# Layer 2 of a four-layer graph kernel: unread products in the two places where TensorE waits

## The chip, the cores and the metric

The kernel runs on one core of one Trainium2 chip. The metric is the device time of one execution in microseconds (us), lower is better. The runs of the kernel before took 1992.58, 1993.73 and 1993.85 us.

## The reference

Four graph layers are computed one after another on 3125 nodes with 256 features and 53125 edges sorted by destination. Each is followed by `x = layernorm(x + layer(x))`. Layer 0 is a normalised graph convolution, layer 1 a weighted sum with two weight matrices, layer 3 a weighted sum after one matrix. Layer 2 is graph attention with four heads of 64 features:

```
z = einsum('nd,hdf->nhf', h, W)
e = leaky_relu(es[src] + ed[dst]);  e = where(e == 0, -1000, e)
m = segment_max(e, dst);  ex = exp(e - m[dst])
denom = segment_sum(ex, dst);  alpha = ex / denom[dst]
out = segment_sum(alpha * z[src], dst)
```

## The kernel before

Every engine has its own hand-written program, and semaphores order them. Layers 0, 1 and 3 go through a dense adjacency matrix, and TensorE multiplies it tile by tile (L1163, L1219). **Layer 2** is different. The edges are taken in 84 groups of 640: 128 partitions by 5 columns (KC = 5). A group touches a window of 48 destination nodes, so four heads make 192 columns (HW).

For one group, GpSimd (POOL in the profile) issues five indirect DMAs (L462), which fetch 128 rows each of the table of transformed source nodes into one of five slots of `ring`. It waits for `slot_free` first, which TensorE raises on the last of its sums for the group that used the slot. VectorE (DVE) makes one-hot matrices (L914) and logits (L920 to L939), masks them (L946), takes the maximum over the columns of each partition (L954), over the partitions (L960), and the running maximum (L969); it subtracts it (L979) and later adds the sums to the accumulator (L1000). ScalarE (ACT) copies the transposed one-hots (L567) and takes the exponentials (L580, L583).

TensorE's loop is software-pipelined. In iteration g, in this order (L1292 to L1305), it does:

- `transpose_max(g)`, L1268, 2 records: turns the partition maxima. It waits for `vmax_ready`, which is DVE's L954. DVE's L960 waits for it.
- `transpose_hots(g + 2)`, L1250, 5 records of 128 bf16 columns. ACT's L567 waits for it.
- `spread_max(g)`, L1277, 4 records. It waits for `mg_ready`, which is DVE's L960 of the same group, and for `mnew_ready` of the group before (L969).
- `sums(g - 1)`, head 0, L1287, 10 records.
- `destination_logits(g + 2)`, L1259, 5 records.
- `sums(g - 1)`, heads 1 to 3, L1287, 30 records. The last raises `slot_free`.

DVE's loop runs beside it in iteration g: masked (L946), new maximum of g - 1 (L969), partition maximum of g (L954), change of the maximum (L975), one-hots of g + 2 (L914), shift (L979), logits (L920), keep (L984), logits (L926), group maximum of g (L960), logits and rescale (L930, L992, L935, L939), add_sums of g - 2 (L1000).

PSUM banks: the sums of group k go to columns 0 to 191 of `sum_banks[k % 3]`, and the spread maximum to columns 0 to 191 of `mb_bank`. Columns 256 to 511 of these banks hold nothing in layer 2. `ident16` is the 128 by 128 identity in bf16.

Of the kernel before, what the change touches and what calls it, by code (L numbers as in the profile page):

```python
# [14 lines left out]
P = 128  # L15
WIN = 48
KC = 5
SLOTS = 5
# [5 lines left out]
NPAN = P // PAN  # L24
HALF = NPAN // 2
QUAD = 4
PAIR = 2
QUADS = NPAN // QUAD
HQ = QUADS // 2
HP = HALF // PAIR  # L30
GRAN = 16
# [8 lines left out]
def gnn_program(nc, x, src, dst, edge_weight, w0, b0, w_rel, b_rel, w_root, w_att, att, w3, b3, out):  # L40
    N, D = x.shape
    E = src.shape[0]
    H, _, F = w_att.shape
# [24 lines left out]
    with ctx:  # L68
        def sb(name, shape, dt=F32):
            return ctx.enter_context(nc.sbuf_tensor(name, shape, dt))  # L70

        def sem(name):
            return ctx.enter_context(nc.semaphore(name))
# [9 lines left out]
        ident16 = sb("ident16", [P, P], BF16)  # L83
# [54 lines left out]
        def carver(whole):  # L138
            at = [0]

            def carve(parts, *dims, dt=F32):
                n = int(np.prod(dims))
                words = n if dt in (F32, I32) else -(-n // 2)
                v = whole[0:parts, at[0]:at[0] + words]
                at[0] += words
                if dt != F32:
                    v = v.bitcast(dt)[:, 0:n]
                if len(dims) > 1:
                    names = "abcdef"[:len(dims)]
                    v = v.rearrange(f"p ({' '.join(names)}) -> p {' '.join(names)}", **dict(zip(names, dims)))  # L150
                return v
            return carve
# [44 lines left out]
        carve(P, NPAD)  # L197
        iota2 = carve(P, P, PAIR, dt=BF16)
        digs = [carve(P, 5, HALF, dt=BF16) for _ in range(2)]
# [7 lines left out]
        carve = carver(work)  # L207
        oh = [(carve(P, HP, P, PAIR, dt=BF16), carve(P, HP, NT * PAN, PAIR, dt=BF16),
               carve(P, 3, HP, NT * PAN, PAIR, dt=BF16)) for _ in range(2)]

# [22 lines left out]
        sum_banks = (banks[0], banks[1], banks[7])  # L233
        ed_bank, vmaxT_bank, mb_bank = banks[4], banks[5], banks[6]
# [35 lines left out]
        y = {n: sem(f"L2_{n}") for n in (  # L270
            "slot_free", "hot_ready", "added", "based", "moved", "relok", "pen_ready", "hotT_ps", "hotT_ready", "ed_ps", "lg",
            "val_ready", "vmax_ready", "vmaxT", "mg_ready", "mb", "mnew_ready", "dm_ready", "rm_ready",
            "shifted", "resc_ready", "prob_ready", "accmul")}
# [7 lines left out]
        def has(g):  # L281
            return 0 <= g < GROUPS

        def uses(r, g):
            return r * len(range(g % SLOTS, GROUPS, SLOTS)) + g // SLOTS + 1
# [119 lines left out]
        def _(pool):  # L405
            G = nc.gpsimd
            G.iota(ident[:], [[1, P]], base=0, channel_multiplier=-1, allow_small_or_imprecise_dtypes=True)
            G.iota(iota2, [[1, P], [0, PAIR]], base=0, channel_multiplier=0,
                   allow_small_or_imprecise_dtypes=True)
# [58 lines left out]
        def _(act):  # L468
# [34 lines left out]
            def counts(i, q):  # L503
                act.wait_ge(c_quad, i * QUADS + (q + 1))
                S.copy(ac[:, :, q * QUAD * PAN:(q + 1) * QUAD * PAN],  # L505
                       cnt_banks[q % 2][:, 0:NT * QUAD * PAN].rearrange("p (b d) -> p b d", b=NT)).then_inc(c_cev, 1)

# [106 lines left out]
        def _(dve):  # L614
# [60 lines left out]
            def numbers(width):  # L675
                return iota2[:, 0:width].unsqueeze(1).to_broadcast([P, HP, width, PAIR])

# [124 lines left out]
            def add_weights(t, i, q, r):  # L802
                dve.wait_ge(c_quad, i * QUADS + (q + 1))
                dve.wait_ge(c_wad, i * QUADS + (q + 1))
                part = aw[t % 2][:, :, q * QUAD * PAN:(q + 1) * QUAD * PAN]
                V.scalar_tensor_tensor(out=part, in0=part, scalar=keep[:, bass.ds(r, 1)],  # L806
                                       in1=w_banks[q % 2][:, 0:NT * QUAD * PAN].rearrange("p (b d) -> p b d", b=NT),
                                       op0=ALU.mult, op1=ALU.add).then_inc(c_wad, 1)
# [250 lines left out]
        def _(pe):  # L1059
            mm = nc.tensor.matmul  # L1060
# [13 lines left out]
            for c in range(CGRP):  # L1074
                ins = mm(banks[5][0:NPAN, 0:NT], gq_lo[:, c, :], gq_hi[:, c, :], start=(c == 0), stop=(c == CGRP - 1),
                         skip_group_check=True)
# [16 lines left out]
            for m, w in enumerate((wrel_r, wroot_r)):  # L1093
# [11 lines left out]
               start=True, stop=True).then_inc(s_bb, 1)  # L1105
# [36 lines left out]
            def adjacency(i, q):  # L1142
# [5 lines left out]
                lo, code, wtd = oh[h]  # L1148
                for k in range(QUAD):
                    cols = slice(k * PAN, (k + 1) * PAN)  # L1150
# [38 lines left out]
            for t in range(NT + 2):  # L1189
                if t < NT:  # L1190
                    if t >= 2:
                        pe.wait_ge(e0["u"], t - 1)
                    for j in range(3):
                        mm(out_banks[t % 2][:, 0:D], ident16[:, :], y0p[:, t, j, :], start=(j == 0), stop=False,
                           skip_group_check=True)
# [44 lines left out]
            def attention_products(r):  # L1240
                def number(k):
                    return r * GROUPS + k

                def transpose_hots(k):
                    s, i = k % SLOTS, number(k)
                    pe.wait_ge(y["hot_ready"], i + 1)
                    pe.wait_ge(y["hotT_ready"], i + 1)
                    pe.sem_inc(held, 1)
                    for c in range(KC):
                        ins = T(hotT_bank[:, c, 0:EP], hot16[:, s, c, :], ident16[0:EP, 0:EP])  # L1250
                    ins.then_inc(y["hotT_ps"], 1)

                def destination_logits(k):
                    s, i = k % SLOTS, number(k)
                    pe.wait_ge(y["hotT_ready"], i + 2)
                    pe.wait_ge(edw_loaded[s], 16 * uses(r, k))
                    pe.wait_ge(y["lg"], 5 * i + 1)
                    for c in range(KC):
                        ins = mm(ed_bank[0:EP, c * PARTS * H:(c + 1) * PARTS * H], hotT[:, c, :], edw[:, s, :].bitcast(BF16),  # L1259
                                 start=True, stop=True)  # L1260
                    ins.then_inc(y["ed_ps"], 1)

                def transpose_max(k):
                    i = number(k)
                    pe.wait_ge(y["vmax_ready"], i + 1)
                    pe.wait_ge(y["mg_ready"], i + 1)
                    for j in range(2):
                        ins = T(vmaxT_bank[0:2 * WIN, j * EP:(j + 1) * EP], vmax[:, j * 2 * WIN:(j + 1) * 2 * WIN],  # L1268
                                ident[0:EP, 0:EP])
                    ins.then_inc(y["vmaxT"], 1)  # L1270

                def spread_max(k):
                    i = number(k)
                    pe.wait_ge(y["mg_ready"], i + 2)
                    pe.wait_ge(y["mnew_ready"], i + 1)
                    for j in range(2):
                        ins = mm(mb_bank[:, j * 2 * WIN:(j + 1) * 2 * WIN], mg[:, j:j + 1].to_broadcast([2 * WIN, P]),  # L1277
                                 ident[0:2 * WIN, 0:2 * WIN], start=True, stop=True, skip_group_check=True)
                    ins.then_inc(y["mb"], 1)

                def sums(k, heads):
                    s, i = k % SLOTS, number(k)
                    pe.wait_ge(y["prob_ready"], i + 4)
                    pe.wait_ge(y["added"], i + SLOTS - 1)
                    for h in heads:
                        for c in range(KC):
                            ins = mm(sum_banks[k % 3][0:FH, h * WIN:(h + 1) * WIN], rows[0:EP, s, c, h * FH:(h + 1) * FH],  # L1287
                                     prob[:, k % 2, c, h * WIN:(h + 1) * WIN], start=(c == 0), stop=(c == KC - 1))
                    if h == H - 1:
                        ins.then_inc(y["slot_free"], 1)  # L1290

                for g in range(-2, GROUPS + 1):  # L1292
                    if has(g):
                        transpose_max(g)
                    if has(g + 2):
                        transpose_hots(g + 2)
                    if has(g):
                        spread_max(g)
                    if has(g - 1):
                        sums(g - 1, range(0, 1))  # L1300
                    if has(g + 2):
                        destination_logits(g + 2)
                    if has(g - 1):
                        sums(g - 1, range(1, H))
# [13 lines left out]
            with pe.Fori(0, nsw) as r:  # L1318
                attention_products(r)
# [12 lines left out]
            for t in range(NT + 3):  # L1332
# [4 lines left out]
                if t >= 3:  # L1337
                    k = t - 3
# [30 lines left out]
```

## Time and profile before

| | |
|---|---|
| runs of the kernel before | 1992.58, 1993.73, 1993.85 us (median 1993.73) |
| profiled execution, its own time | 1987.39 us |
| its span, first to last instruction | 1985.6 us |
| mean granted TensorE clock over the span | 0.828 |
| layer 2 in the trace | about 937 to 1643 us, 84 groups |

Durations are read from the one profiled execution. Its time is 1.8 us more than its span, and 6.3 us less than the median of the runs. In the profile, PE is TensorE's products and PEld its weight loads, which overlap. PEclk is the clock that TensorE was granted: 1.0 is 2.4 GHz and 0.5 is 1.2 GHz; a mean between them is a mixture of the two.

### The profile page before, as it was taken

Reading aid. Unit: us, or ns where it says so; the run is one execution under the profiler, and the core shown is the slowest. Engines: PE = TensorE matmul, PEld = TensorE weight load, DVE = VectorE, ACT = ScalarE, POOL = GpSimd, SP = SyncE. Lnnn points to the kernel's source line nnn. Section 1 sums busy time; section 2 is a strip of 40 time slices with the busy share of each in tenths; the row PEclk is TensorE's granted clock in tenths of the full one; section 3 lists DMA queues with packets and bytes.
Section 4 is the critical chain, followed back from the end, with each engine's and each line's share of the span. In section 5 each row is a group of like instructions: output and inputs, shape, how many; then the busy total and the mean of one; then the engine's idle time right before and its main releaser. Section 6 shows DMA issues by size and latency. Waiting matters only on the chain.

```text
span 1985.6 us, 37417 instructions
## 1 busy us (share of the span) xinstructions
PE 1685.3 (85%) x13647; PEld 1458.5 (73%) x13647; DVE 1245.3 (63%) x2739; ACT 448.6 (23%) x996; POOL 645.0 (32%) x539
## 2 busy tenths in 40 slices
PE   5568999899998999997388888887888887899998
PEld 4347777777776888886277777777777775788887
DVE  8568989889896111222488887788888788321211
ACT  0242232322221000102132233332233325200000
POOL 0034443455452000001455555555555530000000
PEclk9889999999999999998556555556555567999999
DMA  7902212122124344441233333333333322244441
GB/s 124 111 11 103 103 71 103 71 103 100 74 104 197 113 145 144 144 145 58 76 85 88 88 88 88 88 85 88 88 88 88 88 57 100 105 153 169 170 152 45
DMA packets 75841, 203.58 MB, mean 103 GB/s; under 512 B 37259, under 2 KB 51951, under 8 KB 66063
## 3 DMA queue, kind: packets, MB, share of 16 engines
q1 hardware_dynamic: 54671, 141.84, 22.2%
q0 software_dynamic: 20992, 59.37, 11.4%
q8 instruction: 112, 1.84, 0.4%
q14 instruction: 66, 0.54, 0.1%
HBM read 152.90 MB, written 53.57 MB: 104 GB/s over the span
## 4 chain that ended last, share of the span: by engine, by line
PE 69%; DVE 13%; issue 7%; SPq 3%; another core or an unknown queue 3%; ACT 2%; DVEq 1%; DMA 1%; ACTq 0%
PE bank L1219 27%; PE bank L1287 13%; PE bank L1163 10%; PE bank L1268 5%; PE bank L1155 4%; PE bank L1277 3%; PE bank L1181 2%; SPq L321 2%; PE bank L1152 2%; DVE big L806 2%; DVE work L979 1%; DVE work L960 1%; PE bank L1227 1%; DVE x_sb L817 1%
## 5 line engine op out<-in xcount | busy, mean ns | idle before, releaser
L462 POOL DMA_INDIRECT ring<-attention_rows,work x420 | 398.5, 949 | 304.8 <-remote 161.3
L1287 PE MATMUL bank<-work,ring 128*65 128x48 f32 x3360 | 382.6, 299 | 0.0
L1287 PEld LDWEIGHTS bank<-work,ring 128*65 128x65 f32 x3360 | 368.3, 220 | 1.8
L1219 PE MATMUL bank<-big,ring 128*128 128x256 f32 x1250 | 273.0, 379 | 1.4 <-DVE x_sb L832 1.4
L1219 PE MATMUL bank<-big 128*128 128x256 f32 x1250 | 272.9, 379 | 0.0
L1219 PEld LDWEIGHTS bank<-big,ring 128*128 128x128 f32 x1250 | 236.5, 190 | 33.8 <-DVE x_sb L832 2.2
L1219 PEld LDWEIGHTS bank<-big 128*128 128x128 f32 x1250 | 236.6, 190 | 31.7
L1163 PE MATMUL bank<-big 128*128 128x256 bf16 x1875 | 209.0, 273 | 14.6 <-ACT big L505 14.6
L1163 PEld LDWEIGHTS bank<-big 128*128 128x128 bf16 x1875 | 181.4, 98 | 39.0 <-ACT big L505 18.3
L1277 PE MATMUL bank<-ident,work 96*128 96x96 f32 x336 | 86.0, 402 | 116.0 <-DVE work L960 113.4
L1152 PE MATMUL bank<-work 128*128 128x100 bf16 x800 | 153.3, 211 | 21.9 <-DVE big L806 14.2
L1277 PEld LDWEIGHTS bank<-ident,work 96*128 96x128 f32 x336 | 67.5, 281 | 137.8 <-DVE work L960 135.1
L1155 PE MATMUL bank<-work 128*128 128x100 bf16 x2400 | 162.7, 210 | 0.0
L510 ACT ACTIVATE std<-mv,epsc 128x1 f32<-128x1 f32 x100 | 29.5, 295 | 553.1 <-DVE mv L812 552.8
L954 DVE TENSOR_REDUCE work<-work 128x192 f32<-128x960 f32 x84 | 154.5, 1839 | 0.0
L1155 PEld LDWEIGHTS bank<-work 128*128 128x128 bf16 x2400 | 151.5, 99 | 0.1
L793 DVE TENSOR_TENSOR work<-work,ring 128x1600 bf16<-128x1600 bf16 x156 | 148.2, 990 | 0.0
L806 DVE SCALAR_TENSOR_TENSOR big<-big,ring,bank 128x400 f32<-128x400 f32 x200 | 122.9, 627 | 35.5 <-PE bank L1155 33.2
L1048 DVE TENSOR_TENSOR u<-bank,bias 128x256 f32<-128x256 f32 x25 | 10.6, 425 | 211.4 <-PE bank L1219 211.4
L434 POOL TENSOR_TENSOR ring<-ring 32x128 bf16<-32x128 bf16 x26 | 129.6, 4984 | 2.2
L505 ACT CAST big<-bank 128x400 bf16<-128x400 f32 x200 | 98.5, 493 | 107.8 <-PE bank L1155 107.8
L960 DVE TENSOR_REDUCE work<-bank 96x2 f32<-96x256 f32 x84 | 35.3, 421 | 119.6 <-PE bank L1268 82.4
(211 smaller groups left out, 2065.2 us busy)
## 6 DMA issues: line engine op xcount, KB each, us to landing
adjacency<-big SPq DMA_DIRECT2D x25, 1600.0 KB, 5.2
ring<-adjacency SPq DMA_DIRECT2D x25, 1600.0 KB, 7.2
big<-adjacency SPq DMA_DIRECT2D x25, 1600.0 KB, 7.3
ring<-attention_rows,work POOLq DMA_INDIRECT x420
edge_rows<-edge_list SPq DMA_DIRECT2D x1, 4983.0 KB
x_sb<-in_x SPq DMA_DIRECT2D x1, 3072.0 KB
out_x<-xnT SPq DMA_DIRECT2D x24, 128.0 KB, 4.3
attention_rows<-ring SPq DMA_DIRECT2D x13, 135.0 KB, 2.3
```

The costliest lines, as they stand in the source:

```text
L434: G.tensor_tensor(raw[:, :, CODE], raw[:, :, CODE], off, ALU.add).then_inc(c_raw, 1)
L462: G.indirect_dma_start(out=rows[0:EP, s, c, 0:ZG], out_offset=None, in_=ztab[:, :], in_offset=bass.IndirectOffsetOnAxis(ap=idx[:, g, c:c + ...
L793: ins = V.tensor_tensor(oh[h][2][:, j], oh[h][1], repeated(digs[h][:, W1 + j], NT * PAN), ALU.mult)
L806: V.scalar_tensor_tensor(out=part, in0=part, scalar=keep[:, bass.ds(r, 1)], in1=w_banks[q % 2][:, 0:NT * QUAD * PAN].rearrange("p (b d) -> ...
L954: V.tensor_reduce(vmax[:], val[:, k % 3].rearrange("p c w -> p w c"), AX_X, ALU.max).then_inc(y["vmax_ready"], 1)
L1152: mm(cnt_banks[b][:, 0:NT * QUAD * PAN].rearrange("p (b d) -> p b d", b=NT)[:, :, cols], lo[:, g, :, m], code[:, g, :, m].rearrange("p (b ...
L1155: ins = mm(w_banks[b][:, 0:NT * QUAD * PAN].rearrange("p (b d) -> p b d", b=NT)[:, :, cols], lo[:, g, :, m], wtd[:, j, g, :, m].rearrange( ...
L1163: ins = mm(out_banks[t % 2][:, 0:D], ac[:, b, :], y0p[:, b, j, :], start=False, stop=False, skip_group_check=True)
L1219: ins = mm(bank[:, 0:D], slots[s][:, b, :], ybuf[:, b, :], start=(b == 0), stop=(b == NT - 1))
L1268: ins = T(vmaxT_bank[0:2 * WIN, j * EP:(j + 1) * EP], vmax[:, j * 2 * WIN:(j + 1) * 2 * WIN], ident[0:EP, 0:EP])
L1277: ins = mm(mb_bank[:, j * 2 * WIN:(j + 1) * 2 * WIN], mg[:, j:j + 1].to_broadcast([2 * WIN, P]), ident[0:2 * WIN, 0:2 * WIN], start=True, ...
L1287: ins = mm(sum_banks[k % 3][0:FH, h * WIN:(h + 1) * WIN], rows[0:EP, s, c, h * FH:(h + 1) * FH], prob[:, k % 2, c, h * WIN:(h + 1) * WIN], ...
```

## The change

Five products are put in front of `transpose_max` and five in front of `spread_max`. Each multiplies the bf16 identity by itself, read twice side by side (256 columns), into columns 256 to 511 of a bank. Nothing reads the result. The first five go to the bank that the sums of this group will use, after a wait for the accumulator's add of group k - 3, which had read that bank; the second five go to `mb_bank` after a wait for the new maximum of the group before.

```diff
+STREAMS = 5
...
+                idle_cols = ident16[:, :].unsqueeze(1).to_broadcast([P, 2, P])
+
+                def stream(bank):
+                    for _ in range(STREAMS):
+                        mm(bank[:, 2 * P:4 * P].rearrange("p (a b) -> p a b", a=2), ident16[:, :], idle_cols, start=True, stop=True,
+                           skip_group_check=True)
+
+                def stream_to_sums(k):
+                    pe.wait_ge(y["added"], number(k) + SLOTS - 2)
+                    stream(sum_banks[k % 3])
+
+                def stream_to_spread(k):
+                    pe.wait_ge(y["mnew_ready"], number(k) + 1)
+                    stream(mb_bank)
...
                 for g in range(-2, GROUPS + 1):
                     if has(g):
+                        stream_to_sums(g)
                         transpose_max(g)
                     if has(g + 2):
                         transpose_hots(g + 2)
                     if has(g):
+                        stream_to_spread(g)
                         spread_max(g)
```

## Rows read from the trace of the kernel before

**Rows 1.** The page: busy time by engine; the granted clock in 40 slices.
```profile
PE 1685.3 (85%) x13647; PEld 1458.5 (73%) x13647; DVE 1245.3 (63%) x2739; ACT 448.6 (23%) x996; POOL 645.0 (32%) x539
...
PEclk9889999999999999998556555556555567999999
```

**Rows 2.** The chain of work, 1140 to 1240 us, shares by line.
```profile
by line: PE bank L1287 39.7%; PE bank L1268 14.7%; issue 12.0%; PE bank L1277 9.4%; DVE work L979 4.6%; another core or an unknown queue 4.5%; DVE work L960 3.7%; PE bank L1259 1.8%; DVE work L975 1.4%; DVEq L906 1.3%; DVE work L946 0.9%; D
```

**Rows 3.** Windows: stretch, length; PE, PEld, DVE, ACT, POOL busy; PEclk, DMA, GB/s.
```profile
992.24:1620.59 628.35, 516.08 (x4369) 461.18 (x4369) 508.35 (x1172) 191.18 (x313) 369.66 (x390) 0.57 0.33 87
...
1169.72:1177.77 8.05, 7.01 (x57) 6.29 (x57) 6.51 (x17) 2.45 (x5) 4.74 (x5) 0.50 0.33 88
1193.84:1201.89 8.05, 6.08 (x57) 5.23 (x57) 6.50 (x17) 2.44 (x5) 4.74 (x5) 0.60 0.31 86
984.43:992.24 7.81, 4.80 (x56) 3.82 (x57) 6.51 (x17) 2.78 (x5) 4.66 (x5) 0.89 0.35 89
1620.59:1626.80 6.21, 5.35 (x52) 4.84 (x52) 6.18 (x16) 1.95 (x4) 0.00 (x0) 0.62 0.24 26
```

**Rows 4.** Half-clock group by time: start, length, work, [idle before <-who ended it].
```profile
1162.19 0.34 DVE L1000 TENSOR_TENSOR big<-big,bank 65x192 f32 x1
...
1163.52 0.35 DVE L969 TENSOR_TENSOR bank<-big,bank 128x192 f32<-128x192 f32 x1
1163.78 1.84 DVE L954 TENSOR_REDUCE work<-work 128x192 f32<-128x960 f32 x1
...
1167.40 0.63 PE L1268 MATMUL bank<-ident,work 128*96 128x128 f32 x2
...
1167.96 0.73 PE L1250 MATMUL bank<-ident,work 128*48 128x128 bf16 x5
1169.24 0.42 DVE L960 TENSOR_REDUCE work<-bank 96x2 f32<-96x256 f32 x1 [1.50 <-PE bank L1268]
1169.38 0.69 ACT L567 COPY work<-bank 48x640 bf16<-48x640 bf16 x1 [1.08 <-PE bank L1250]
...
1169.72 1.17 PE L1277 MATMUL bank<-ident,work 96*128 96x96 f32 x4 [1.03 <-DVE work L960]
...
1169.98 0.95 POOL L462 DMA_INDIRECT ring<-attention_rows,work  x1 [2.09 <-remote]
```

**Rows 5.** Timeline of a group that began at the full clock.
```profile
1193.84 0.68 PE L1277 MATMUL bank<-ident,work 96*128 96x96 f32 x4 [1.33 <-DVE work L960]
...
1198.48 0.63 PE L1268 MATMUL bank<-ident,work 128*96 128x128 f32 x2
...
1201.42 0.42 DVE L960 TENSOR_REDUCE work<-bank 96x2 f32<-96x256 f32 x1 [1.52 <-remote]
...
1201.89 1.17 PE L1277 MATMUL bank<-ident,work 96*128 96x96 f32 x4 [1.90 <-DVE work L960]
```

**Rows 6.** Waits, 992 to 1620 us: total, times, longest.
```profile
PE bank L1277 <- DVE work L960: 109.6, 78, 2.7
```

**Rows 7.** Windows inside layer 2, columns as in rows 3.
```profile
1099.50:1103.00 3.50, 3.50 (x32) 3.37 (x32) 3.50 (x7) 0.79 (x2) 2.58 (x4) 0.50 0.40 109
1103.50:1105.00 1.50, 0.19 (x4) 0.02 (x1) 0.18 (x1) 0.11 (x2) 0.00 (x0) 1.00 0.37 98
1107.00:1110.00 3.00, 3.00 (x30) 3.00 (x29) 3.00 (x6) 0.36 (x1) 2.39 (x3) 0.50 0.45 116
```

**Rows 8.** TensorE at full clock: 256-column bf16 products, then five transposes of 128.
```profile
184.74 7.48 PE L1163 MATMUL bank<-big 128*128 128x256 bf16 x67
...
1192.05 0.46 PE L1250 MATMUL bank<-ident,work 128*48 128x128 bf16 x5
```

**Rows 9.** TensorE: one transpose held up while gathers are issued.
```profile
990.76 0.27 PE L1250 MATMUL bank<-ident,work 128*48 128x128 bf16 x1 [1.24 <-issue]
```

**Rows 10.** Timeline at the start of layer 2, and at its end.
```profile
973.01 0.36 DVE L969 TENSOR_TENSOR bank<-big,bank 128x192 f32<-128x192 f32 x1 [17.93 <-remote]
...
1634.23 8.97 PE L1287 MATMUL bank<-work,ring 128*65 128x48 f32 x80
```

## The prediction

> **What bounds the kernel now.** I read the page first. TensorE is busy 1685.3 us, and its granted clock falls to 5 and 6 tenths in layer 2 while it is near full elsewhere [rows 1]. So the question is what half a clock costs there. The chain of waits over a hundred microseconds of the layer gives TensorE most of the time: L1287 alone has 39.7% [rows 2]. Read alone, that says TensorE bounds the layer and a faster clock would pay.
>
> The windows say otherwise. From 992.24 to 1620.59 us there are 78 groups in 628.35 us: 8.06 us each, with 6.62 us of TensorE (516.08 / 78) and 6.52 us of DVE (508.35 / 78) [rows 3]. A group at clock 0.50 takes 8.05 us and has 7.01 us of TensorE. A group at a mean clock of 0.60 has 6.08 us of TensorE and takes 8.05 us too. One at 0.89 has 4.80 us and takes 7.81 us, and it is the first in which the gathers run again [rows 3]. TensorE's work fell by 0.93 us and the period did not move. The timeline shows where the time went: in the group that began at the full clock L1268 starts 4.64 us after L1277 instead of 5.72, but L1277 of the next group starts 3.41 us after L1268 instead of 2.32 [rows 4, 5]. TensorE only waits longer for L960.
>
> What does L960 wait for? The trace names L1268, or nobody it knows. At half clock L1268 ends at 1168.03 and L960 starts at 1169.24; in the other group L1268 ends at 1199.11 and L960 starts at 1201.42, 2.3 us later [rows 4, 5]. In both, L960 starts at the same place of an 8.05 us beat. ACT's L567, which waits for another TensorE signal, starts 0.14 us after L960, and POOL, which waits for a third (`slot_free`), 0.74 us after it [rows 4]. Three signals that TensorE finished at different moments become visible together. The beat looks like POOL's own: five gathers at 1.25 us, then a gap of 2.09 us [rows 4] (4.74 us busy per group [rows 3]). Where POOL issues nothing, a group takes 6.21 us with 6.18 us of DVE [rows 3]. So I take the layer to be paced by the gathers: TensorE's signals of a group show only when POOL's five gathers are issued, and POOL starts the next five on one of these signals. TensorE's clock is not in that loop.
>
> **The change, part by part.** Nothing is removed. Each group gets ten products (and weight loads) on TensorE and two waits.
>
> *Price of five products.* At the full clock 67 products of this form take 7.48 us; less the 0.27 us tail of the last that is 0.109 us each, 0.55 us for five [rows 8]. At half clock no product of this width is in the trace. The five transposes, of half its columns, take 0.73 us against 0.46 us at the full clock [rows 4, 8]; without a tail of about 0.3 us in the slow case that is 0.105 us each, so about 0.21 us for twice the columns. Doubling 0.109 gives 0.218. I take 1.07 us for five, with 0.55 and 1.09 us as the ends.
>
> *Place 1, before L1268.* At half clock there is no wait here: L1268 starts at 1167.40 as the sums end, though DVE's L954 was done at 1165.62 [rows 4]. The five products push it by 1.07 us, to an end at 1169.10. L960 began at 1169.24, so it still just fits. At the full clock the sums end long before the next beat and the products cost nothing.
>
> *Place 2, before L1277.* The 1.03 us of idle before L1277 [rows 4] takes most of 1.07 us, but L1250 now also ends 1.07 us later. With TensorE at half clock all through, a group would have 7.01 + 2.14 = 9.15 us of TensorE and no idle. At the full clock it would have 4.80 + 1.10 = 5.90 us [rows 3, 8] of a beat of 8.05.
>
> *The added waits.* The accumulator's add that place 1 waits for lies three groups back; even the latest one before L1268, L1000, started 5.2 us before it. The new maximum of place 2, L969, ends at 1163.87, 4.1 us before L1250 begins [rows 4]. Both are met. What is queued behind them is TensorE's own order, and it doesn't wait. Cost 0. The other queues issue nothing new.
>
> *The clock.* After 3.50 us of TensorE without a gap the clock was 1.00; after 1.50 us at that level with 0.19 us of work by 1107 us it was 0.50 again [rows 7]. So long busy stretches raise it and the idle before L1277 loses it. With the products a half-clock group has no idle left, so the clock should rise much more often; at the full clock some 2 us of idle per group stay (8.05 - 5.90), so it should still fall. TensorE keeps the beat if it has the full clock for a share f with f / 5.90 + (1 - f) / 9.15 = 1 / 8.05, that is f = 0.25, a mean clock of 0.62; it has 0.57 now [rows 3]. I expect about 0.75, halfway between the levels, so TensorE keeps up, and DVE's 1.5 us of slack per group (8.05 - 6.52) absorbs a late L1268.
>
> The Trainium skill, "TensorE: Matmul & The Clock Gate", section "HAM oscillation", prices a throttled stretch at its length times one half, as work that would all come back. For 628 us at a mean of 0.57 that is an estimate of 270 us gained (628 x 0.86 x 0.5). The two groups of 8.05 us at different clocks disagree with it, by that rule a fall of 0.9 us in busy time should have shortened the group.
>
> *Ends of the layer.* At the start the first products lie in long idle, before a DVE wait of 17.93 us [rows 10]: 0 to 2 us. At the end 80 sums run for 8.97 us at half clock [rows 10]; if the full clock happens to be granted then, at TensorE's share of 4.80 / 7.01 they take 6.1 us: 0 to 3 us gained. I take 0 for both together.
>
> **Sum.** 78 beats times 0, and 0 at the ends: 1987.39 us for the profiled execution, as before. The median of the runs stands 6.3 us above the profiled time and goes with it: 1993.7, which I give as 1994 us.
>
> **Rivals.**
>
> *Faster: TensorE is the bound.* For it: the chain [rows 2], and 109.6 us of waits of L1277 for L960 in 78 groups [rows 6], which might be paid back if the sums and L1268 came early in every group. Then DVE is next at 6.52 us, and the layer loses 78 x (8.06 - 6.52) = 120 us: 1874 us. A weaker form is that signals that come early enough sometimes escape the gathers. Against: in the group of 4.80 us TensorE work the next L1277 still came 7.81 us later. Chance 0.15.
>
> *Slower: the clock stays low.* If products of an identity by itself don't lift the clock, TensorE becomes the bound with 9.15 us a group: 78 x 1.10 = 86 us, 2080 us. It decides where the mean clock of the layer stays under 0.62. For it: the third window, fully busy at half clock and still there at its end [rows 7]. Against: all idle would be gone. Chance 0.10.
>
> *Slower by a little: TensorE comes late in some groups.* In a half-clock group L1277 starts about 1.15 us late. And while gathers are issued TensorE can't run far ahead: one transpose was held 1.24 us with nothing to wait for [rows 9]. Ten more instructions may pile up there and start only after the release, in front of L1277. If one group in ten to one in three misses DVE's slack by 0.5 to 1 us, it is 4 to 25 us: some 2005 us. Chance 0.18.
>
> *The change doesn't do what it says:* the clock rises only a little and the time stays. It is part of my case.
>
> **Numbers.** No change 0.57. What a measurement can tell from no change is about 0.2%, 4 us. Faster 0.15, slower 0.28 (0.10 and 0.18). The range takes my case with the ends of the layer (plus or minus 4 us), a faint gain, and the small loss: 1985 to 2018 us. My case alone is 1989 to 1998 us.
>
> **What would show it.** Right: L1277 to L1277 still 8.05 us in steady groups at either clock; a mean clock near 0.75 in the layer; L567 still 0.14 us after L960 and POOL 0.74 us after it; TensorE's idle still before L1277. Wrong: periods under 8 us with the gathers running (the beat is not POOL's own), or groups of over 8.5 us with no idle on TensorE (the clock did not rise), or L1268 starting after the beat.

## The result, and the profile after

| | before | after |
|---|---|---|
| median of 4 runs | 1993.15 us | 2019.34 us (2017.0 to 2021.29) |
| ratio, 95% interval | | 1.0132 [1.0115, 1.015] |
| profiled execution, its own time | 1987.39 us | 2018.6 us |
| mean granted clock over the span | 0.828 | 0.910 |

The change makes the kernel slower by 1.3%, with the forecast at no change, and 1 us outside its range. Yet the clock rose, as it was meant to.

The page of the kernel after (line numbers have moved: L960 is now L961, L1250 L1251, L1268 L1269, L1277 L1278, L1287 L1303, L462 L463; the ten products are L1286). First its span, clock and the chain's shares by engine, then the groups of POOL's gathers and of the sums:

```profile
span 2016.8 us, 39097 instructions
...
PEclk9889999999999999996788888877877778999999
...
PE 74%; issue 12%; DVE 8%; SPq 3%; ACT 2%; DMA 1%; DVEq 0%; another core or an unknown queue 0%; ACTq 0%
...
L463 POOL DMA_INDIRECT ring<-attention_rows,work x420 | 401.0, 955 | 338.7 <-PE bank L1303 210.4
L1303 PE MATMUL bank<-work,ring 128*65 128x48 f32 x3360 | 295.2, 237 | 145.2 <-issue 143.2
```

Layer 2's slices show 7 and 8 tenths where [rows 1] had 5 and 6. New is the last line: TensorE stood still for 145.2 us in front of its sums, and for 143.2 of them it waited for nothing that the profile shows. And POOL's wait is now put down to the sums, by name.

The window that answers to [rows 3] runs from the 9th L961 to the 77th, 68 groups:

```profile
core 0: us, PE busy (x) PEld busy (x) DVE busy (x) ACT busy (x) POOL busy (x), PEclk, DMA share, GB/s
1031.80:1611.40 579.60, 455.84 (x4490) 382.71 (x4491) 451.56 (x1021) 166.38 (x272) 324.03 (x340) 0.81 0.31 83
```

That is 579.60 / 68 = 8.52 us a group, against 8.06 before, at a mean clock of 0.81 against 0.57. 68 groups by 0.46 us is 31 us, all of the difference of the two profiled executions (2018.6 - 1987.39 = 31.2). TensorE is busy 6.70 us of a group, DVE 6.64: neither is the bound.

The waits from 1000 to 1620 us (engine, line and what it waited for: us in total, times, longest):

```profile
POOL ring L463 <- PE bank L1303: 182.2, 72, 3.2
...
PE bank L1303 <- issue: 133.5, 207, 1.2
...
DVE work L961 <- PE bank L1269: 69.6, 68, 2.0
```

L1278's wait for L961 [rows 6] is gone. In its place TensorE is held 207 times inside the sums, almost three times a group. The timeline of TensorE shows one of these groups and the next:

```profile
start us, us, engine line op out<-in xcount [idle before <-releaser]
1201.98 0.46 PE L1251 MATMUL bank<-ident,work 128*48 128x128 bf16 x5
1202.37 0.72 PE L1286 MATMUL bank<-ident 128*128 128x256 bf16 x5
1202.93 0.58 PE L1278 MATMUL bank<-ident,work 96*128 96x96 f32 x4
1203.35 0.74 PE L1303 MATMUL bank<-work,ring 128*65 128x48 f32 x10
1204.02 0.28 PE L1260 MATMUL bank<-work 48*128 48x12 bf16 x5
1204.23 1.26 PE L1303 MATMUL bank<-work,ring 128*65 128x48 f32 x18
1205.73 0.20 PE L1303 MATMUL bank<-work,ring 128*65 128x48 f32 x1 [0.24 <-issue]
1206.45 0.30 PE L1303 MATMUL bank<-work,ring 128*65 128x48 f32 x2 [0.51 <-issue]
1207.87 0.27 PE L1303 MATMUL bank<-work,ring 128*65 128x48 f32 x2 [1.12 <-issue]
1208.58 0.24 PE L1303 MATMUL bank<-work,ring 128*65 128x48 f32 x1 [0.45 <-issue]
1209.30 0.88 PE L1303 MATMUL bank<-work,ring 128*65 128x48 f32 x6 [0.48 <-issue]
...
1215.38 1.85 PE L1303 MATMUL bank<-work,ring 128*65 128x48 f32 x28
1218.20 0.30 PE L1303 MATMUL bank<-work,ring 128*65 128x48 f32 x2 [0.97 <-issue]
```

And POOL's over the same stretch (the first and the last gather of each five):

```profile
1202.13 0.94 POOL L463 DMA_INDIRECT ring<-attention_rows,work  x1 [2.23 <-PE bank L1303]
...
1207.13 0.95 POOL L463 DMA_INDIRECT ring<-attention_rows,work  x1 [0.30 <-issue]
1211.00 0.94 POOL L463 DMA_INDIRECT ring<-attention_rows,work  x1 [2.92 <-PE bank L1303]
...
1216.11 0.95 POOL L463 DMA_INDIRECT ring<-attention_rows,work  x1 [0.30 <-issue]
1219.32 0.94 POOL L463 DMA_INDIRECT ring<-attention_rows,work  x1 [2.26 <-PE bank L1303]
```

The gathers begin at 1202.13. TensorE runs without a gap until 1205.49, with 18 of the last 30 sums done; then sums pass one or two at a time, at instants 0.71 us or twice that apart (1205.73, 1206.45, 1207.87, 1208.58, 1209.30). The last sum, which raises `slot_free`, is done near 1210.2 instead of before the gathers end at 1208.08. POOL's next five start 8.87 us after the last five (1211.00 - 1202.13), the five after them 8.32 us later. Before, that interval was the beat of 8.05.

How long after the last sum POOL starts tells the two kernels apart. After: the last sums end at 1210.18 (1209.30 + 0.88) and 1218.50 (1218.20 + 0.30), and POOL starts at 1211.00 and 1219.32, 0.82 us later both times. In the kernel before the last sum ends 5.67 us after the first gather of [rows 4], at 1175.65, still while gathers are issued, and POOL starts only 2.38 us later:

```profile
1172.11 3.54 PE L1287 MATMUL bank<-work,ring 128*65 128x48 f32 x30
1174.99 0.95 POOL L462 DMA_INDIRECT ring<-attention_rows,work  x1 [0.30 <-issue]
1178.03 0.95 POOL L462 DMA_INDIRECT ring<-attention_rows,work  x1 [2.09 <-remote]
```

The same holds group by group from 1000 to 1600 us, where a sum counts as held after a gap of over 0.15 us. Before, no sum is held in any of 75, and POOL starts 2.3 us or more after the last. After, sums are held in 67 of 70 (in the other three TensorE is at half clock with no gap), and POOL starts 0.81 to 1.13 us after the last. `slot_free` went from being early to being what POOL waits for.

A group in which the clock never rose (L961 at 1313.61 to L961 at 1322.51):

```profile
1313.61:1322.51 8.90, 8.90 (x68) 7.74 (x69) 6.68 (x16) 2.45 (x4) 4.85 (x6) 0.50 0.30 80
```

8.90 us, TensorE without a gap: here it is the bound, as forecast (9.15). Only four groups after 1000 us are like this.

### The profile page after: what moved, and what is told of

The parts are those of the page before. It is cut to its first block, busy times and chain, and to the rows that moved or that the text cites. A ratio compares the mean times of both kernels' runs of the same rounds, so it can differ in the third digit from the quotient of the medians.

```text
span 2016.8 us, 39097 instructions
## 1 busy us (share of the span) xinstructions
PE 1694.8 (84%) x14487; PEld 1433.8 (71%) x14487; DVE 1255.3 (62%) x2739; ACT 448.1 (22%) x996; POOL 641.4 (32%) x539
## 4 chain that ended last, share of the span: by engine, by line
PE 74%; issue 12%; DVE 8%; SPq 3%; ACT 2%; DMA 1%; DVEq 0%; another core or an unknown queue 0%; ACTq 0%
PE bank L1220 27%; PE bank L1303 13%; PE bank L1164 10%; PE bank L1286 7%; PE bank L1156 4%; PE bank L1278 2%; PE bank L1251 2%; PE bank L1182 2%; PE bank L1153 2%; DVE big L807 2%; SPq L322 2%; PE bank L1269 1%; PE bank L1228 1%; DVE x_sb L818 1%; PE bank L1260 1%
## 5 line engine op out<-in xcount | busy, mean ns | idle before, releaser
L463 POOL DMA_INDIRECT ring<-attention_rows,work x420 | 401.0, 955 | 338.7 <-PE bank L1303 210.4
L1303 PE MATMUL bank<-work,ring 128*65 128x48 f32 x3360 | 295.2, 237 | 145.2 <-issue 143.2
L1303 PEld LDWEIGHTS bank<-work,ring 128*65 128x65 f32 x3360 | 259.8, 153 | 169.1 <-issue 165.8
L1286 PE MATMUL bank<-ident 128*128 128x256 bf16 x840 | 166.6, 347 | 0.0
L435 POOL TENSOR_TENSOR ring<-ring 32x128 bf16<-32x128 bf16 x26 | 136.1, 5233 | 2.2
L1286 PEld LDWEIGHTS bank<-ident 128*128 128x128 bf16 x840 | 89.3, 121 | 31.4 <-issue 9.3
L426 POOL DMA_INDIRECT ring<-edge_rows,cur x26 | 37.0, 1422 | 221.0 <-PE bank L1140 220.8
```

The source lines that it names most:

```text
L435: G.tensor_tensor(raw[:, :, CODE], raw[:, :, CODE], off, ALU.add).then_inc(c_raw, 1)
L463: G.indirect_dma_start(out=rows[0:EP, s, c, 0:ZG], out_offset=None, in_=ztab[:, :], in_offset=bass.IndirectOffsetOnAxis(ap=idx[:, g, c:c + ...
L1286: mm(bank[:, 2 * P:4 * P].rearrange("p (a b) -> p a b", a=2), ident16[:, :], idle_cols, start=True, stop=True, skip_group_check=True)
```

## The experiments

Eighteen runs, some of the same kernel, in five comparisons. Each comparison is on one chip, and the chips turned out to differ: the kernel before takes 1868 to 1872 us on three of them (*free* below) and 1983 to 1995 us on the others (B, C and the one of the result, which may be one of these two). I call those *holding* chips; why, the runs show. "Groups" counts L960 (its counterpart) from 1000 to 1400 us in the trace, "clock" is the mean granted one there.

| run | chip | kernel | us | ratio to before on that chip | groups | clock |
|---|---|---|---|---|---|---|
| before | result's | | 1993.15 | 1 | 50 | 0.57 |
| after | result's | | 2019.34 | 1.0132 [1.0115, 1.015] | 47 | 0.83 |
| e1 | A, free | place 1 alone | 1866.71 | 0.9992 [0.9982, 1.0001] | 59 | 0.86 |
| e2 | A | place 2 alone | 1841.03 | 0.9857 [0.984, 0.9873] | 61 | 0.92 |
| e3 | A | both, 16 columns | 1888.76 | 1.0111 [1.0094, 1.0128] | 56 | 0.57 |
| e4 | A | before, 10 small ones ahead of the sums | 1876.63 | 1.0053 [1.0036, 1.0069] | 58 | 0.71 |
| e5 | B, holding | before | 1994.81 | 0.9999 [0.9988, 1.001] | 49 | 0.56 |
| e6 | B | after | 2022.34 | 1.013 [1.0112, 1.0148] | 47 | 0.83 |
| e7 | B | before, SyncE's loads | 1869.2 | 0.9369 [0.9353, 0.9386] | 59 | 0.56 |
| e8 | B | place 2 alone | 1993.23 | 0.9992 [0.9982, 1.0002] | 49 | 0.65 |
| e9 | C, holding | place 1 alone | 1983.04 | 1.0 [0.999, 1.0009] | 49 | 0.73 |
| e10 | C | both, 16 columns | 1993.34 | 1.0053 [1.0037, 1.007] | 49 | 0.50 |
| e11 | C | as e4 | 2020.33 | 1.0191 [1.0174, 1.0208] | 48 | 0.50 |
| e12 | C | after | 2006.4 | 1.0117 [1.0094, 1.0139] | 48 | 0.81 |
| e13 | D, free | before, SyncE's loads | 1868.19 | 0.9984 [0.9974, 0.9993] | 59 | 0.56 |
| e14 | D | after, SyncE's loads | 1840.57 | 0.9837 [0.982, 0.9853] | 61 | 0.98 |
| e15 | D | ten in place 2 | 1838.77 | 0.9829 [0.9813, 0.9845] | 62 | 1.00 |
| e16 | D | after | 1841.61 | 0.9842 [0.9826, 0.9859] | 61 | 1.00 |
| e17 | E, free | ten in place 2 | 1836.71 | 0.9834 [0.9818, 0.9851] | 61 | 1.00 |
| e18 | E | after, SyncE's loads | 1839.91 | 0.9845 [0.9829, 0.9862] | 62 | 1.00 |

**One place at a time, fewer columns, more instructions (e1 to e4).**

```diff
 e1, against after:
-                        stream_to_spread(g)
 e2, against after:
-                        stream_to_sums(g)
 e3, against after:
-                idle_cols = ident16[:, :].unsqueeze(1).to_broadcast([P, 2, P])
+                idle_cols = ident16[:, 0:8].unsqueeze(1).to_broadcast([P, 2, 8])
 e4, against before, in sums():
+                    if 0 in heads:
+                        for _ in range(10):
+                            mm(sum_banks[k % 3][:, 2 * P:2 * P + 16], ident16[:, :], ident16[:, 0:16], start=True, stop=True,
+                               skip_group_check=True)
```

> Only the five products before L1268 (TensorE's turn of the partition maxima) stay; the other five are gone. Count theory (while GpSimd issues its five gathers TensorE can only get a limited number of instructions ahead, so instructions that lie between the start of the gathers and the last of the sums hold slot_free back): these five lie behind the sums in TensorE's order, so 0 to 10 us over the kernel before, 1993 to 2003 us. Time theory (the products' own columns make TensorE late): half of the changed kernel's 26 us, some 2006 us.

> Only the five products before L1277, ahead of the sums, stay. Count theory: they share the stretch of the gathers with the sums, so most of the loss is here: 2010 to 2020 us. Time theory: half of it, some 2006 us; or none, since at half clock they fit into TensorE's idle before L1277: 1993 us.

> Both places, the same ten products and ten weight loads a group, but 16 columns wide instead of 256. Count theory: the instructions alone cost: 2005 to 2020 us, if they meet the gathers; near 1993 us only if, at the half clock that then stays (mean clock of the layer near 0.57), they are issued before the gathers start. Time theory: 16 times fewer columns, so no loss, 1993 to 1996 us. Clock theory (the full clock itself brings the loss, because TensorE then runs into the limit sooner): clock stays low, no loss, 1993 to 1996 us.

> The kernel before, with ten products of 16 columns right before the first head of the sums: 20 more TensorE instructions a group inside the stretch of the gathers, with 0.3 to 0.5 us of time against 1.0 us of idle a group. Count theory: the last sums are held until the gathers are issued and come after that: periods of 8.5 to 9.5 us instead of 8.05, 2025 to 2100 us. Time theory and clock theory: within TensorE's idle, so 1993 to 1998 us.

This chip takes 1868.61 us for the kernel before, and nothing in the expectations fits such a chip. What it shows is another bound: groups take 6.6 to 7.1 us (400 by 61 to 56), so POOL's beat isn't there. Place 2 alone pays 1.4%, place 1 alone nothing. The 16-column products of e3 leave the clock at 0.57 and cost 1.1%: on this chip TensorE at that clock is the bound (in e3 busy 385.66 of the 400 us), and products that don't lift the clock are work added to it. In e4 the clock is 0.71 and the cost 0.5%; why small products in that place come with a higher clock no run shows. So my theories had to be tried on the other kind of chip.

**The same on a holding chip, and the gathers taken from GpSimd (e5 to e8).** In e7 SyncE loads the rows with plain transfers of the same size from consecutive rows; the gather by index is left out.

```diff
 in SyncE's program, for each group:
+                    sp.wait_ge(y["slot_free"], r * GROUPS + (g + 1))
+                    for c in range(KC):
+                        sp.dma_start(rows[0:EP, s, c, 0:ZG], ztab[c * P:(c + 1) * P, :]).then_inc(gathered[s], 16)
 in GpSimd's program:
-                        G.indirect_dma_start(
```

> The kernel before, unchanged, for its trace on the chip of this call. In the call before this one it took 1868 us where the given runs have 1993. Chip theory (on some chips TensorE's signals are held while GpSimd issues its gathers, on others not): either 1993 us with steady groups of 8.05 us and POOL starting 0.7 us after L960, or 1868 us with groups of 6.5 to 7.3 us that follow TensorE's clock. A theory of one chip, on which the beat is always 8.05 us, falls with the second.

> The changed kernel on the chip of this call. Where the kernel before takes 1993 us: 2019 us again, 1.3% slower. Where it takes 1868 us: count theory and clock theory say there is nothing to hold TensorE back, so the clock rises and the group is bound by TensorE's 5.9 us at full clock or DVE's 6.5: 1840 to 1865 us, 0 to 1.5% faster. Time theory: half-clock groups of 8.9 us mixed with 6.5: slower, 1880 to 1930 us.

> The kernel before with the same number and size of row loads into the same slots, issued by SyncE as plain transfers of consecutive rows instead of by GpSimd's indirect ones: the gather by index is left out. On a chip with 8.05 us groups: if GpSimd's issuing holds the signals, groups fall to 6.5 to 7.1 us and the time to 1870 to 1910 us; if the transfers themselves do, it stays near 1993 us. On a chip with 1868 us: no change within 10 us by either.

> The five products before L1277 alone, again. On a chip with 1868 us: 1841 us as before. On a chip with 1993 us: count theory 2005 to 2020 us, time theory 1993 to 2006 us.

The loss of the whole change repeats (1.013). With the same bytes moved by SyncE's transfers the kernel before falls from 1994.93 to 1869.2 us, the time that free chips give with GpSimd's gathers. One window of that trace:

```profile
core 0: us, PE busy (x) PEld busy (x) DVE busy (x) ACT busy (x) POOL busy (x), PEclk, DMA share, GB/s
1200.00:1300.00 100.00, 97.77 (x818) 88.62 (x819) 95.07 (x221) 35.43 (x59) 0.00 (x0) 0.54 0.36 101
```

POOL is busy 0.00 us, more bytes move per us than before (101 against 87 GB/s), and TensorE at half clock is the bound (97.77 of 100 us). So it is GpSimd's indirect gathers that make the beat of 8.05 us, and not the bytes moved. e7 changes two things at once, who issues the loads and whether their rows are picked by index; that the issuing is what counts is argued, not shown. Place 2 alone costs nothing here (0.9992), and gains nothing. The count theory had put most of the loss there (2005 to 2020 us, measured 1993.23): that was a miss.

**Place 1, the narrow ones and e4 on a holding chip (e9 to e12).** Same edits.

> The five products before L1268 alone, again. Chips differ: one has the kernel before at 1868 us, two at 1993 to 1995 us. On a chip of the second kind, with place 2 alone at no change, place 1 must carry the changed kernel's loss: 2010 to 2025 us, with gaps inside the sums and slot_free late in every second group. If instead both places are needed for the loss: 1993 to 2000 us. On a chip of the first kind: 1867 us as before.

> Both places, 16 columns instead of 256, so the same instructions and hardly any column time, and the clock stays at half. Chip of the second kind: count theory (TensorE can get only so many instructions ahead while the gathers are issued, and place 1 adds ten of them behind the sums) 2005 to 2025 us; clock theory (the loss needs the full clock, at which TensorE reaches the limit earlier) 1993 to 1998 us. Chip of the first kind: 1889 us again.

> The kernel before with ten products of 16 columns (20 instructions) right before the sums. Chip of the second kind: count theory 2010 us and more, since these are in the way of slot_free; clock theory 1993 to 2000 us. Chip of the first kind: 1877 us again.

> The changed kernel on the chip of this call. Chip of the second kind: 2019 to 2022 us. Chip of the first kind, not yet tried: place 2 alone gave 27 us there by a full clock and place 1 alone none, so with DVE's 6.5 us as the floor of a group 1835 to 1870 us; 1890 us and more would mean that the columns of both places together cost TensorE time there.

Place 1 alone costs nothing either (1.0), where 2010 to 2025 us was expected should it carry the loss: each place is free (e8 on B, e9 on C), the two together cost 1.2% (e12). And e11 costs most of all, with the clock at 0.50 throughout and products that take 0.46 us of a group. Its timeline of TensorE, one group:

```profile
1206.86 1.17 PE L1277 MATMUL bank<-ident,work 96*128 96x96 f32 x4
1207.82 0.46 PE L1287 MATMUL bank<-ident 128*128 128x16 bf16 x10
1208.13 1.31 PE L1291 MATMUL bank<-work,ring 128*65 128x48 f32 x10
1209.38 0.29 PE L1259 MATMUL bank<-work 48*128 48x12 bf16 x5
1209.61 3.15 PE L1291 MATMUL bank<-work,ring 128*65 128x48 f32 x25
1213.00 0.24 PE L1291 MATMUL bank<-work,ring 128*65 128x48 f32 x1 [0.25 <-issue]
1213.71 0.67 PE L1291 MATMUL bank<-work,ring 128*65 128x48 f32 x4 [0.47 <-issue]
```

and POOL's (L462, the gathers):

```profile
1206.65 0.95 POOL L462 DMA_INDIRECT ring<-attention_rows,work  x1 [2.59 <-PE bank L1291]
...
1215.19 0.95 POOL L462 DMA_INDIRECT ring<-attention_rows,work  x1 [2.58 <-PE bank L1291]
```

From the start of the gathers (1206.65) 4 + 10 + 10 + 5 + 25 = 54 products begin before TensorE is held, and 5 sums stay behind. Without the ten, the last sum is the 49th product (4 + 10 + 5 + 30) and gets through. So neither wide columns nor a raised clock is needed for a loss. It comes when the last sum falls behind the point at which TensorE is held.

What sets that point is open. In the group of the kernel after that begins at 1202.13, at the full clock, it is 44 products (the last two of L1251's five, then 5 + 4 + 10 + 5 + 18), 3.36 us after the first gather. In the next one it is 59 from 1211.00 to the 28th sum, 6.2 us after it, and two stay behind. That group begins at half clock but has the full one for its last sums (28 of them in 1.85 us, where e11 needs 3.15 us for 25). From 1000 to 1600 us the 32 groups of the kernel after that stay at the full clock up to that point are held after 44 to 48 products and 3.36 to 3.81 us. e9 has 24 such groups, held after 49 to 56 products and 3.6 to 4.8 us, and e11, at half clock, is held after 50 to 60 products and 5.5 to 6.7 us. Neither one number of products nor one time fits all of these. For e11 either would do: its ten products also take 0.46 us, and the last sum, which ends 5.67 us after the first gather in the kernel before, comes after 6.1 us with them.

e9 shows the harmless case, place 1 alone at the full clock, with gathers from 1199.70:

```profile
1200.89 1.97 PE L1303 MATMUL bank<-work,ring 128*65 128x48 f32 x30
1202.70 0.85 PE L1286 MATMUL bank<-ident 128*128 128x256 bf16 x5
1203.90 0.38 PE L1269 MATMUL bank<-ident,work 128*96 128x128 f32 x2 [0.35 <-issue]
1205.37 0.22 PE L1251 MATMUL bank<-ident,work 128*48 128x128 bf16 x1 [1.09 <-issue]
```

All 30 sums are through before TensorE is held; it is held in the transposes behind them, and L961 keeps its beat (8.06 us in that group, from 1199.01 to 1207.07).

e10 has the instructions of the whole change without its columns. It costs 0.53%, where the whole costs 1.17% on that chip, about 10 us: more than the clock theory's 0 to 5, less than the count theory's 12 at least. It is not the same loss at half the size. From 1000 to 1600 us the sums are held in 17 of its 73 groups only; in the other 56 the last sum passes and TensorE is held in the products of place 1 right behind it:

```profile
1203.09 3.54 PE L1303 MATMUL bank<-work,ring 128*65 128x48 f32 x30
1206.42 0.21 PE L1286 MATMUL bank<-ident 128*128 128x16 bf16 x1
1207.34 0.27 PE L1286 MATMUL bank<-ident 128*128 128x16 bf16 x4 [0.70 <-issue]
```

From gathers to gathers these 56 groups take 8.16 us on the mean and the 17 take 8.23, against 8.07 in e9 on the same chip. Most of e10's small loss comes without held sums, and its cause is open. What the 256 columns and the raised clock do each, no run separates.

**Is the change good where nothing holds TensorE? (e13 to e18)** e15 has `STREAMS = 10` and no `stream_to_sums`; e14 and e18 are the change with e7's loads (the gather by index left out).

> The kernel before with the rows of the gathers loaded by SyncE's plain transfers of consecutive rows (the gather by index is left out). Both theories: about 1869 us, as it was in the run before this one, whatever the chip; groups of 6.8 us, paced by TensorE at a mostly low clock. It is the base for the next run.

> The kernel after with the same plain loads (the gather by index left out). Theory A (the change costs only because TensorE can get a limited number of instructions ahead while GpSimd issues the gathers): without GpSimd's issuing nothing is held, the clock rises and the groups go to DVE's 6.5 us, so it is not slower than its base and up to 1.5% faster: 1840 to 1870 us. Theory B (the products cost by themselves, through their banks, their waits or their columns): 1% or more slower than its base, 1890 us.

> All ten products in front of the spread of the maximum, none in front of its transpose: the same number of instructions and columns as the change. If the number of instructions ahead of the last sums decides: slower as the change is, by 0.8 to 1.5%, on a chip where the kernel before takes 1980 us or more. If it needs both places (the wait for the add, the bank of the sums, a late transpose of the maximum): no change, within 0.2%. On a chip where the kernel before takes 1870 us, the signals are not held and it says little.

> The change as it is, beside the others. On a chip where the kernel before takes 1980 us or more: 1.1 to 1.3% slower, as in the three comparisons so far. On one where it takes 1870 us: by theory A no such loss, 1840 to 1880 us; by theory B 1890 us or more.

> Ten products in front of the spread of the maximum alone. On a chip where the kernel before takes 1980 us or more: if the number of instructions decides, 0.8 to 1.5% slower, with TensorE held in the sums in every second group; if it needs both places, no change within 0.2%. On a chip where the kernel before takes 1870 us: 1.7% faster, as in the run before.

> The change with SyncE's plain loads in place of GpSimd's gathers (the gather by index left out). Theory A (only GpSimd's issuing makes the change cost): 1841 us on any chip, so 7 to 8% under the kernel before where that takes 1980 us or more, and 1.5% under the 1869 us of the plain loads without the change. Theory B: 1890 us or more there.

Both comparisons ran on free chips. The whole change, 1.2 to 1.3% slower in three comparisons on holding chips, is 1.6% faster here (e16). One window of its trace, gathers by GpSimd:

```profile
core 0: us, PE busy (x) PEld busy (x) DVE busy (x) ACT busy (x) POOL busy (x), PEclk, DMA share, GB/s
1200.00:1300.00 100.00, 84.20 (x1038) 68.68 (x1036) 99.36 (x229) 35.56 (x62) 73.30 (x78) 1.00 0.41 109
```

and of its timeline:

```profile
1206.00 0.69 PE L1278 MATMUL bank<-ident,work 96*128 96x96 f32 x4 [0.90 <-DVE work L961]
1206.53 0.74 PE L1303 MATMUL bank<-work,ring 128*65 128x48 f32 x10
...
1207.41 1.97 PE L1303 MATMUL bank<-work,ring 128*65 128x48 f32 x30
```

The full clock is kept through the window (1.00), all sums pass without a gap while POOL is 73% busy with gathers, and DVE is the bound at 99.36 of 100 us. Theory B of the expectations (the products cost by themselves) is out for free chips: e14, e16 and e18 agree with theory A. GpSimd's gathers cost next to nothing there: e13 takes 0.16% less than the kernel before. Where the ten stand makes no difference there (0.9829 in place 2, 0.9842 in both).

Left open: ten in place 2, and the whole change with SyncE's loads, on a holding chip. Both were run twice, on free ones. So it is not shown whether ten products in one place would cost what five in each of the two do, and that the change would pay on a holding chip without GpSimd's gathers is only inferred from e7 and e14. What differs between the chips no run shows.

No version tried on both kinds of chip beats both kernels on both. Place 2 alone comes nearest: no change on a holding chip (0.9992), 1.4% faster on a free one (0.9857).

## Why the prediction was wrong

*What bounds the kernel.* Right for this chip: the gathers pace the layer at 8.05 us and the clock does not. e7 shows it: the same kernel without GpSimd's gathers takes 125 us less. But I read it as a property of the kernel; it is one of some chips.

*Price of five products.* Right. At half clock five take 1.25 to 1.27 us in the timeline with a tail, against 1.07 without; at the full clock 0.71 to 0.72 us. A group at half clock takes 8.90 us (forecast 9.15). The 5.90 us at the full clock was too high: 4.80 us came from a group at a mean clock of 0.89, and e16 has 334.78 us of TensorE in 61 groups, 5.5 us each, at 1.00.

*The clock.* Right in kind: 0.81 for "about 0.75", well over the 0.62 at which TensorE keeps up by itself. The 0.75 was a midpoint between two levels, so that it came near is in part luck.

*The added waits.* Right, 0: neither is among TensorE's waits from 1000 to 1620 us.

*Place 1 and place 2.* Right one by one (e9 1.0, e8 0.9992), wrong together. **The step that failed** is "TensorE's clock is not in that loop", taken as if nothing that is added to TensorE were in it, and with it the sum "78 beats times 0". The prediction had the loop (POOL starts the next five on `slot_free`) but took the signal to be in time whatever TensorE does, because its busy time per group stayed under 8.05 us. The busy time was never the condition. On a holding chip TensorE is stopped at some product while the gathers are issued, and `slot_free` is in time only if the last sum lies ahead of that stop. In the kernel before it does in all 75 groups, and POOL starts 2.3 us or more after it; in the kernel after sums are held in 67 of 70, and POOL starts some 0.8 us after the last one, 8.52 us after its last start on the mean instead of 8.06. The term "78 beats times 0" measured about 0.46 us a group. I looked at DVE's slack of 1.5 us, which L961 still had, and not at the place of the last sum in TensorE's order.

*The rival that came true* is the small loss. Its mechanism stood there: "Ten more instructions may pile up there and start only after the release." Its size came out at 31 us for 4 to 25: not one group in ten to three but nearly all, by 0.46 us on the mean. And it named the wrong victim: the instructions held are not those in front of L1277 but the sums, and the late signal is `slot_free`. I gave it 0.18, though the held transpose of [rows 9] was the one row that showed TensorE's limit. To follow that stop through TensorE's order would have asked the right question, though it would not have given the size: at the full clock the kernel after is held after 44 to 48 products, e9 after 49 to 56.

*The rival "faster"* (TensorE is the bound, then DVE at 6.52 us a group) did not happen on this chip. On the free ones its end is what happens, 6.5 us a group and DVE 99% busy, but from groups of about 6.8 us (e13, 59 in 400 us) and not of 8.06. *"The clock stays low"* did not happen.

*The Trainium skill's price of a throttled stretch* ("TensorE: Matmul & The Clock Gate", section "HAM oscillation"): half its length comes back. By that rule the rise of the clock from 0.57 to 0.81 should have given an estimated 150 us: (0.81 - 0.57) / 0.5 of some 628 us at half price. The trace disagrees: the layer became 31 us longer. On free chips the time did fall with the clock, by 30 us (e16, from 1871.56 to 1841.61), until DVE took over.

## What to carry to other kernels

Filler work on an idle engine can cost more than its own time: look at what must be issued before the signal that others wait for, and at the places in the trace where the engine stands with "issue" as its only reason. A slack in busy time does not say that the signal is in time. Where GpSimd issues indirect transfers in a loop, put the instruction that frees the next slot early, and fillers behind it (e9: no cost). Before you believe a gain or a loss of 1%, measure on several chips: here it changed its sign.

## What the hardware showed that I had not expected

- The same kernel takes 1868 to 1872 us on three chips and 1983 to 1995 us on at least two others. The whole difference (125 us) goes away when SyncE's plain loads stand in for GpSimd's gathers (1869.2 us on chip B).
- On a holding chip, while gathers are issued, TensorE stops after 44 to 60 products in the traces of the kernel after and of e11 and goes on in steps of about 0.71 us or twice that, often one or two products each. The Trainium skill, "Advanced Engine Details and Errata", section "Engine Queue Depths", gives TensorE a queue of 64 instructions. The counts of products stay under it; with a weight load for each they are 88 to 120 instructions, over it. Neither is constant, and no run here shows that this queue is what fills.
- On a holding chip ten products of 16 columns, 0.46 us of work, cost 37 us (e11 against 1983.43), 0.44 us for each of 84 groups, though TensorE at half clock had idle time for them.
